# Band rows of the skewed softmax stored slot by slot, with all 32 heads inside a slot

## What is computed

```
disp = (x @ W_disp)        # per head, 16 wide
val  = (x @ W_val)         # per head, 8 wide
strain  = disp_win - disp            # 64 window positions for every token
logits  = gelu(strain @ W_strain + rel_emb @ W_pos) @ W_bond
          - 10 * sigmoid(gelu(strain @ W_dmg + b_dmg) @ W_dmg_out + b_dmg_out)
weights = softmax(where(cmask, logits, -inf))      # over the 64 positions
out     = einsum('bntd,bntde->bnte', weights, val_win)
out     = out.transpose(0, 2, 1, 3).reshape(B, T, C) @ W_cproj
```

## Time and profile before

| what | value |
|---|---|
| median of three runs | 1162.64 us |
| lowest, highest run | 1155.72, 1165.59 us |
| span of the profiled execution | 1215.3 us (no other time is given for it) |
| mean granted TensorE clock in it | 0.927 of full speed |
| weigh-and-gather stage, half 0 | about 300 to 379 us of the span |
| weigh-and-gather stage, half 1 | about 634 to 729 us of the span |

### The profile page before, as it was taken

The page is one execution under the profiler, slowest core; times in us unless marked ns, Lnnn a source line. Parts: engine busy times, 40 slices in busy tenths (PEclk is TensorE's granted clock), DMA queues, the critical chain, the costliest instruction groups (busy, mean ns, idle before and its releaser), DMA issues. The chain is left out here.

```text
span 1215.3 us, 24799 instructions
## 1 busy us (share of the span) xinstructions
PE 1012.9 (83%) x9866; PEld 549.0 (45%) x9866; DVE 894.8 (74%) x1046; ACT 790.0 (65%) x851; POOL 563.5 (46%) x569
## 2 busy tenths in 40 slices
PE   6778777889888988888877779986899999998558
PEld 4522222334775333333337776344345656555123
DVE  7888888996648999999959356773685775667137
ACT  3699999998646999999976214311466566554244
POOL 5198887376655588888863005077000000000720
PEclk9799999999699999999997989986799999898679
DMA  8840101120872222222119800002023444321100
GB/s 301 241 160 31 33 33 33 36 69 30 241 159 63 63 72 71 69 70 72 52 43 275 195 2 22 1 25 93 22 79 112 123 124 137 87 79 47 51 25 26
DMA packets 117419, 105.32 MB, mean 87 GB/s; under 512 B 11862, under 2 KB 103666, under 8 KB 116658
## 3 DMA queue, kind: packets, MB, share of 16 engines
q1 hardware_dynamic: 107220, 83.41, 24.1%
q0 software_dynamic: 8512, 20.13, 5.7%
q10 hardware_dynamic: 1571, 0.20, 0.1%
HBM read 62.16 MB, written 38.39 MB: 83 GB/s over the span
## 5 line engine op out<-in xcount | busy, mean ns | idle before, releaser
L261 DVE SCALAR_TENSOR_TENSOR ring<-AD,PT 128x1808 f32<-128x1808 f32 (+15 forms) x128 | 282.9, 2225 | 27.1 <-issue 13.3
L976 PE MATMUL LG<-ring,lred 128*32 128x456 f32 (+15 forms) x2048 | 232.5, 573 | 0.0
L2259 ACT ACTIVATE EX<-SS 128x1024 f32<-128x1024 f32 x128 | 130.8, 1030 | 125.9 <-PE SS L2046 61.8
L2329 DVE TENSOR_REDUCE MX<-SS 128x2 f32<-128x1024 f32 x119 | 144.7, 1219 | 71.1 <-PE SS L2046 52.3
L267 POOL DMA_INDIRECT ys<-rows,goali x80 | 162.2, 2028 | 64.1 <-DVE rows L860 40.5
L916 ACT ACTIVATE ring<-ring 128x3680 f32<-128x3680 f32 (+15 forms) x47 | 161.2, 3430 | 3.6 <-DVE ring L261 3.6
L1001 PE MATMUL SD<-DSf,eyes 99*32 99x456 bf16 (+15 forms) x1280 | 95.2, 374 | 77.6 <-ACT ring L921 66.6
L769 POOL DMA_INDIRECT xs<-rows,sloti x64 | 134.4, 2099 | 30.7 <-issue 19.2
L922 ACT ACTIVATE ring<-ring 128x1824 f32<-128x1824 f32 (+15 forms) x80 | 145.9, 1823 | 0.0
L1963 POOL DMA_INDIRECT XN<-ys,sloti x16 | 16.4, 1024 | 271.7 <-PE SS L2056 267.1
L261 DVE SCALAR_TENSOR_TENSOR ring<-AD,bdmg 128x1808 f32<-128x1808 f32 (+15 forms) x48 | 106.5, 2219 | 0.0
(11 more groups left out here) (419 smaller groups left out, 1767.8 us busy)
## 6 DMA issues: line engine op xcount, KB each, us to landing
w1s<-in_L_ffn_W SPq DMA_DIRECT2D x39, 256.0 KB
w2s<-in_L_ffn_W SPq DMA_DIRECT2D x39, 256.0 KB
band<-ring SPq DMA_DIRECT2D x6, 1024.0 KB, 6.5
xl<-xs SPq DMA_DIRECT2D x20, 272.0 KB, 3.1
xs<-Z SPq DMA_DIRECT2D x5, 1024.0 KB, 8.9
w1s<-w1d SPq DMA_DIRECT2D x80, 64.0 KB
w2s<-w2d SPq DMA_DIRECT2D x80, 64.0 KB
band<-Z SPq DMA_DIRECT2D x4, 1024.0 KB, 9.7
```

What stands on the lines that cost most here:

```text
L261: return v.scalar_tensor_tensor(out=tile[:, s, :, t0:T], in0=AD[:, s, :, j + t0:j + T], scalar=extra, in1=AD[:, s, :, PAD + t0:PAD + T], o ...
L976: mm = pe.matmul(LG[32 * b:32 * b + 32, par, s, t0:T], lred[:, s, n % 4, :], ring[:, slot, s, b, t0:T], start=(n % 4 == 0), stop=(n % 4 == 3))
L2259: act.activation(EX[:, Q % 2, hh:hh + 2, t, :], SS[:, slot, :, :], ACT.Exp, scale=SCALE1).then_inc(freed[slot], 1)
L2329: v.tensor_reduce(MX[:, t, p // 2, hh:hh + 2], pairs_of(b, name), AX.X, ALU.max).then_inc(freed[slot], 1)
```

## The change

Band's rows are ordered slot by slot, with all 32 heads inside a slot: 128 slots of 32 numbers. What a write covers is then one run of 64 slots (8 KB) of each row, and what a read covers is one run of 95 slots (12,160 bytes) for each token, with a row step of 32 numbers less than a row. VectorE's subtraction writes its result in that order (position, then head, so with a step of 32 numbers between the positions of one head), and ScalarE reads and writes in order. TensorE's transposes take a head's matrix with a step of 32 numbers. The computation in two parts of tile 0 stays on VectorE and ScalarE, but its write and its reads are one, which wait for both parts; `written` and `landed` lose their part, and the loops over the parts go.

```
-                        sp.dma_start(band[par].rearrange("p (g r) -> p g r", g=NG)[:, :, 4 * WIN:],
-                                     zeros.rearrange("p q t -> p (q t)").rearrange("p (g r) -> p g r", g=NG)).then_inc(d_zero, 16)
+                        sp.dma_start(band[par][:, 32 * WIN:], zeros.rearrange("p q t -> p (q t)")).then_inc(d_zero, 16)
...
-            wide = [flat.rearrange("p (g r n) -> p g r n", g=NG, r=P) for flat in (slots[1], DSf[:, 0:NG * P * 4], slots[0])]
+            wide = [flat.rearrange("p (r n) -> p r n", n=32) for flat in (slots[1], DSf[:, 0:32 * P], slots[0])]
...
-            zs = slots[3].rearrange("p (a g s n) -> p a g s n", a=2, g=NG, s=WIN)
+            zs = slots[3].rearrange("p (a s n) -> p a s n", a=2, n=32)
...
-            diffs = [... .rearrange("p (n q j) -> p n q j", n=32, j=4) for n in range(2)]
+            diffs = [... .rearrange("p (q j n) -> p q j n", n=32, j=4) for n in range(2)]
...
+            def written(k):
+                return d_out[k], 16 * (g + 1)
+
+            def landed(k, half):
+                return d_in[k][half], 16 * (64 // BLK) * (g + 1)
...
-                        rows = dram_rows(band, (k * P + r0) * 32 * P + 4 * P * f, [[32 * P - 4, BLK], [4 * P, l - f], [1, 4 * SPAN]])
-                        engine.dma_start(wide[k % WIDE][r0:r0 + BLK, f:l, s0:s0 + SPAN, :].rearrange("r g s n -> r g (s n)"), rows
-                                         ).then_inc(landed(k, part, half)[0], 16)
+                    rows = dram_rows(band, (k * P + r0) * 32 * P, [[32 * P - 32, BLK], [1, 32 * SPAN]])
+                    engine.dma_start(wide[k % WIDE][r0:r0 + BLK, s0:s0 + SPAN, :].rearrange("r s n -> r (s n)"), rows
+                                     ).then_inc(landed(k, half)[0], 16)
...
-                    for part, (f, l) in enumerate(parts_of(k)):
-                        sp.wait_ge(ex_ready, 5 * g + (k + 2 if k else part + 1))
-                        sp.dma_start(band[k].rearrange("p (g r) -> p g r", g=NG)[:, f:l, 0:4 * WIN],
-                                     zs[:, k % 2, f:l].rearrange("p g s n -> p g (s n)")).then_inc(written(k, part)[0], 16)
+                    sp.wait_ge(ex_ready, 5 * g + k + 2)
+                    sp.dma_start(band[k][:, 0:32 * WIN], zs[:, k % 2].rearrange("p s n -> p (s n)")).then_inc(written(k)[0], 16)
...
-                        v.tensor_tensor(diffs[par][:, 4 * f:4 * l], zt[:, 4 * f:4 * l],
+                        v.tensor_tensor(diffs[par][:, :, :, 4 * f:4 * l].rearrange("p q j n -> p n q j"), zt[:, 4 * f:4 * l],
...
-                        act.activation(zs[:, k % 2, f:l].rearrange("p g s n -> p g n s"),
-                                       diffs[k % 2].rearrange("p (g n) q j -> p g n (q j)", n=4)[:, f:l], ACT.Exp).then_inc(ex_ready, 1)
+                        act.activation(zs[:, k % 2, :, 4 * f:4 * l],
+                                       diffs[k % 2][:, :, :, 4 * f:4 * l].rearrange("p q j n -> p (q j) n"), ACT.Exp).then_inc(ex_ready, 1)
...
-                            mm = pe.transpose(turned(i)[:, n, :], wide[par][:, i, :, n], ident[:])
+                            mm = pe.transpose(turned(i)[:, n, :], wide[par][:, :, 4 * i + n], ident[:])
```

More of the change, by code:

```diff
@@ L1119, in first_layer @@
             wtT = sb(f"wtT{g}", [P, 32, P], F32, sm)
[L1120 removed]
+            diffs = [wtT[:, 16 * n:16 * n + 16, :].rearrange("p a t -> p (a t)").rearrange("p (q j n) -> p q j n", n=32, j=4) for n in range(2)]
             mx = sb(f"mx{g}", [P, 2, 32], F32, sm)
@@ L1148, in summed, with read @@
                 return ZT[:, 8:12, :] if k % 2 else WB[:, 3]
-            def written(k, part):
-                if k == 0 and part == 0 or 0 < k < NT - 1:
-                    return d_out[k], 16 * (g + 1)
-                return d_out[NT - 1], 32 * g + (32 if k else 16)
-            def landed(k, part, half):
-                each = 16 * (64 // BLK)
-                if k == 0 and part == 0 or 0 < k < NT - 1:
-                    return d_in[k][half], each * (g + 1)
-                return d_in[NT - 1][half], 2 * each * g + (2 * each if k else each)
-            def read(engine, k, half, only=None):
+            def written(k):
+                return d_out[k], 16 * (g + 1)
+            def landed(k, half):
+                return d_in[k][half], 16 * (64 // BLK) * (g + 1)
+            def read(engine, k, half):
                 engine.wait_ge(wide_zero, WIDE * g + min(k, WIDE - 1) + 1)
@@ L1167, in read @@
                     engine.wait_ge(band_pe, 8 * (M0 + k - WIDE + 1))
[L1168 to L1176 removed]
+                engine.wait_ge(*written(k))
+                for s0 in range(0, 64, BLK):
+                    r0 = 64 * half + s0
+                    rows = dram_rows(band, (k * P + r0) * 32 * P, [[32 * P - 32, BLK], [1, 32 * SPAN]])
+                    engine.dma_start(wide[k % WIDE][r0:r0 + BLK, s0:s0 + SPAN, :].rearrange("r s n -> r (s n)"), rows
+                                     ).then_inc(landed(k, half)[0], 16)
             @block.gpsimd
@@ L1211, in _ @@
                 write(0)
-                read(sp, 0, 0, 0)
-                write(1)
-                read(sp, 0, 0, 1)
-                for k in range(2, NT):
+                read(sp, 0, 0)
+                for k in range(1, NT):
                     write(k)
-                    read(sp, k - 1, 0)
+                    if k > 1:
+                        read(sp, k - 1, 0)
                 if g == G - 1:
@@ L1394, in turn @@
                     for i in range(8):
-                        for part, (f, l) in enumerate(parts_of(k)):
-                            if i == f:
-                                for half in range(2):
-                                    pe.wait_ge(*landed(k, part, half))
+                        if i == 0:
+                            for half in range(2):
+                                pe.wait_ge(*landed(k, half))
                         before = max(4 * m + i // 2 - 1, 0)
```

12 lines of the change are left out of this document (2 added, 10 removed).

## The result

With the change the kernel takes 1170.82 us in the median (1158.47 to 1179.17 in 16 runs), beside 1160.76 us for the kernel before on the same chip (1152.21 to 1167.86 in 16 runs). The ratio is 1.0076, with a 95% interval of 1.0050 to 1.0102: slower by 8.8 us, or 5.8 to 11.8. The ratio compares runs in the faster of two states alone (it leaves out three of the 16 with the change), so it is not the quotient of the two medians. The time lies inside the range given, but on the other side of the forecast, which was no change with 1159.5 us. Rival A (VectorE pays for its scattered write) is what happened, at a smaller price than it named.

A forecast was written before the change was run, and what follows sets the result against it. VectorE's 18.4 us chain bounds the weigh, then a fixed filler, then TensorE's own work. ScalarE, VectorE, TensorE and transfers 0, holes -3.1 us: 1162.6 - 3.1 = 1159.5 us; range for 8 in 10, 1151 to 1180 us.

The forecast's parts named there:

- Rival A: Ten subtractions in the weigh: VectorE pays for its scattered write, 13.0 to 19.8 us, so 1172.5 to 1179.3 us; chance 0.20.
- What bounds the kernel: Weigh: VectorE's chain of 18.4 us without holes, then a fixed filler of 7.45 us, set the gather's start.
- rival C: Gather start: at higher clock the filler is shorter and reads end last, so earlier tile 0 gains; 1150.9 us; chance 0.10.
- VectorE, the step that failed: Ten subtractions in the weigh, now writing with a step of 32 numbers: taken as 0, 19.8 us kept for the range.
- the -3.1 us: Gathers: half of TensorE's 6.12 us of idle time without a releaser, expected to go.
- ScalarE: Exponentials in the weigh: 1.9 and 1.03 us in order, 16.1 us less over both halves, worth nothing on the path.
- TensorE: Weight loads of band's 256 transposes, step 4 to 32: taken as 0, 17.7 us kept as the possible cost.
- Rival B: Band's transposes: TensorE's weight loads pay more at step 32 than at step 4, 17.7 us, so 1177.2 us; chance 0.08.
- Transfers: Band's writes and reads, 20 instead of 25 a half: taken as 0, 2 x 1.1 us kept for a late tile 0.
- The holes: Gathers: five TensorE stops without a releaser, 6.12 us; earlier and fewer runs thin them by half, -3.1 us.
- Rival D: Weigh: ScalarE's exponential stays at 3.9 us; 1164.8 us at most, no change; chance 0.06.
- The range of the likeliest case: Whole kernel: the forecast's own case, chance 0.56, given as 1153 to 1169 us.

The follow-up runs named there:

- dve_only: Kernel before, with only VectorE's subtraction writing with a step of 32 and ScalarE writing in order; 1169.06 us, ratio 1.0083.
- act_scatters: Changed kernel, but VectorE writes head by head in order and ScalarE's exponential writes slot order with a step of 32; 1161.40 us, ratio 1.002.
- psum_steps: Changed kernel, but VectorE reads PSUM with a step of four numbers and writes slot order in order; 1163.02 us, ratio 1.0043.
- psum_again: psum_steps measured once more, unchanged; 1164.76 us, ratio 1.000 to the kernel before.
- psum_short: psum_steps with a filler of 8 instead of 20 pairs of matmuls ahead of the first turn; 1166.93 us, ratio 1.0062 to the kernel before.

## Why the prediction was wrong

*What bounds the kernel.* Right: VectorE's chain without holes, then the filler. dve_only moved the time through VectorE's chain, and the three kernels without the maximum moved it back. The filler is fixed in its instructions only: its length goes with the granted clock (7.37 us at 0.62, 4.73 at 1.00, as rival C reckoned).

*VectorE, the step that failed.* The prediction put VectorE's stepped write at 0; the runs show 10.5 us in its place (3.61 instead of 2.29 us for 2048 numbers), on a path without slack. It took the 0 from a row of 274 ns for 64 numbers with a step of 32, because 64 numbers in order came out at 278 ns. The in-order rows it used (L651 and L261) belong to forms with other operands and another fixed cost: L651's scalar is a column of gates, that of the 274 ns row a constant. Two rows of the kernel before that have a constant scalar and go in order:

```profile
L816 DVE SCALAR_TENSOR_TENSOR chosen_key<-PH,chosen_key 128x256 f32<-128x256 f32 x1 | 0.4, 425 | 2.2 <-PE PH L1025 2.2
...
L853 DVE SCALAR_TENSOR_TENSOR xg<-attT,xg 128x512 f32<-128x512 f32 x20 | 13.7, 687 | 2.8 <-ACT attT L938 2.8
```

By these a number costs 1.02 ns, and 64 of them 425 - 192 x 1.02 = 229 ns. So the row of 274 ns was 45 ns dearer than in order, 0.70 ns a number. (It also reads one operand with that step, and no run prices such a read on VectorE, so it could only have hinted at the price of the write.) With 0.70 x 2048 x 4 x 2 = 11.5 us the sum would have been near 1162.6 - 3.1 + 11.5 = 1171 us, and the forecast slower; measured were 0.64 ns a number and 10.5 us. That this comes out so near to the measured 1170.8 is in part luck, since the -3.1 us in it did not come. Rival A saw the mechanism and its place, but took the price from ScalarE: a subtraction as long as ScalarE's exponential (3.91 us) or 2.06 times as long as in order, so 13.0 to 19.8 us. The Trainium skill's rule of 16-byte lines (SBUF — State Buffer, section "Door 1: The DMA port swizzle"), set against the 274 ns in the prediction, pointed the right way for both engines: VectorE began to pay (2.29 to 3.61 us) and ScalarE stopped (3.91 to 1.91).

*ScalarE.* Right in size (1.91 and 1.06 us) and in worth: act_scatters and psum_steps differ in ScalarE by a factor of two and not in their time by more than the intervals.

*TensorE.* Taken as 0; the loads became 15 ns cheaper, at most 256 x 0.015 = 3.8 us. Rival B fell. The prediction's "nothing gets nearer to order by a wider step" was wrong as a reason, without consequence; why the wider step is cheaper stays open.

*Transfers.* Right: no transpose waits for tile 0. Its estimate of 1.1 us late at the crowded medians was too dark: it took a median of tiles 2 and 3 for tile 0. In the trace with the change tile 0's write takes 3.9 us, not 6.5, SyncE's two reads 4.3 and 5.7, not 14.4, and GpSimd's last read lands at 322.8 us, 8.9 us ahead of the first transpose. Rival C, which needed the reads to be late, fell with this.

*The holes.* Not thinned: 6.71 us after 6.12, so the -3.1 us didn't come. Their sum is 6.0 us in dve_only, with the old layout, and 6.6, 8.8 and 7.7 in act_scatters, psum_steps and psum_again, with the new one; one execution each, so whether the new layout lengthens them stays open. What the traces do show is that the holes have fixed places in TensorE's program. The first one in the gather of half 0 stands behind the 54th of the 128 matmuls with the values in the kernel before and behind the 55th with the change (73 are left), the first one in that of half 1 behind the 41st and the 42nd. In psum_short, whose filler is 24 of the trace's matmuls shorter in each half, they stand behind the 79th and the 90th:

```profile
337.05 1.59 PE L1413 MATMUL WB<-wtT,ring 128*32 128x64 f32 x49 [3.19 <-issue]
...
674.71 1.24 PE L1413 MATMUL WB<-wtT,ring 128*32 128x64 f32 x38 [5.16 <-issue]
```

That is 24 and 48 matmuls later, by as many as the program has fewer up to there, and in half 1 of psum_steps the holes follow each other after 127 or 128 matmuls. So they hang on the count of TensorE's instructions, and inside these groups the program waits for nothing; this fits the prediction's reading of instructions that come late. How long each hole lasts (0.2 to 5.2 us) changes from kernel to kernel and was not traced to a transfer.

*Rival D* fell: the exponential does what the change says.

*The range of the likeliest case* was added up wrongly: 1162.6 + 6.1 + 2.2 + 3 is 1173.9 us, not 1169. The measured 1170.8 us would lie inside it, but by luck, with the subtractions at 3.61 us that this case had at 2.29.

## What to carry to other kernels

Price a stepped access on the engine that does it, by the slope of its own operation's rows with the same kind of operands; a short row compared with another form hides the price in its fixed cost. When a layout must be turned on the way from PSUM, let VectorE read PSUM with the step and write SBUF in order, or leave a step in SBUF to an engine with time to spare; here either took the loss away and neither brought a gain. Moving work from an engine that waits to the one that sets the pace lost here, although the first one won more than the other lost, and before counting on a shorter chain look for what stands right behind it.

## What was not expected of the hardware

- VectorE's fp32 write to SBUF with a step costs 0.57 to 0.70 ns a number, from 128 numbers on and alike for a step of 4 and of 32; its read of PSUM with a step of 4 costs nothing over one in runs of four (2292 beside 2291 ns for 2048 numbers).
- ScalarE pays for the step on either side in SBUF: 3794 ns reading, 3774 writing, 1910 in order, for 2048 numbers. Reading runs of four numbers with gaps between them is free (1911).
- TensorE's weight load takes 194 ns with a step of 32 numbers, 209 with a step of four.
- A filler of matmuls that looked like waste is worth its 4 us: with 16 instead of 40 of them both kernels were slower, by 0.6 and 1.0%, and in their traces the gather of half 1 went from 65.6 to 76 us, at granted clocks of 0.84 and 0.82 where 0.95 and 0.92 stood.
- TensorE's holes without a releaser keep their places in its instruction stream, 127 or 128 matmuls apart in half 1, and move by as many matmuls as are taken out ahead of them.
